# A message-passing layer on one core: a fourth scatter table, and the remainders of two of five dense groups made on VectorE

## The reference

```python
h = jnp.maximum(_layernorm(x, axis=-1), 0.0)
row, col = src, dst
msg = jnp.concatenate([h[col], edge_attr], axis=1)
msg = jnp.maximum(msg @ W1a + b1a, 0.0) @ W1b + b1b
summed = jax.ops.segment_sum(msg, row, num_segments=6250)
counts = jax.ops.segment_sum(ones, row, num_segments=6250)
agg = summed / jnp.maximum(counts, 1.0)[:, None]
out = x + jnp.maximum(jnp.concatenate([h, agg], axis=1) @ W2a + b2a, 0.0) @ W2b + b2b
```

## Time and profile before

| | |
|---|---|
| three timed runs, median (lowest, highest) | 1560.24 us (1558.22, 1563.16) |
| the profiled execution | 1549.54 us, span 1548.0 us |
| TensorE busy, matmuls | 1460.7 us (94%) x31106 |
| TensorE busy, weight loads | 1395.6 us (90%) |
| VectorE busy | 1413.5 us (91%) |
| ScalarE busy | 1027.4 us (66%) |
| GpSimd busy | 1214.8 us (78%) |
| granted TensorE clock, mean | 0.981 of full speed |

### The profile page before, as it was taken

The page is one execution under the profiler, slowest core; times in us unless marked ns, Lnnn a source line. Parts: engine busy times, 40 slices in busy tenths (PEclk is TensorE's granted clock), DMA queues, the critical chain, the costliest instruction groups (busy, mean ns, idle before and its releaser), DMA issues. The chain is left out here.

```text
span 1548.0 us, 76249 instructions
## 1 busy us (share of the span) xinstructions
PE 1460.7 (94%) x31106; PEld 1395.6 (90%) x31106; DVE 1413.5 (91%) x4756; ACT 1027.4 (66%) x2192; POOL 1214.8 (78%) x803
## 2 busy tenths in 40 slices
PE   3589999999999999999999999999999999999977
PEld 2368999999999999999999999999999999999975
DVE  8778999999999999999999999999999989999977
ACT  5287666776767676666667766666776666676605
POOL 4378888888788888888888888888888888888754
PEclk8699999999999999999999999999999999999998
DMA  5777767767677777777677767676676767677743
GB/s 167 268 135 129 121 111 113 124 113 122 108 125 111 125 112 113 121 107 125 110 123 113 124 110 115 115 122 112 112 123 113 119 104 125 112 119 114 116 82 110
DMA packets 279671, 187.44 MB, mean 121 GB/s; under 512 B 190687, under 2 KB 275548, under 8 KB 278553
## 3 DMA queue, kind: packets, MB, share of 16 engines
q1 hardware_dynamic: 174342, 153.22, 40.5%
q0 software_dynamic: 104976, 29.30, 27.8%
HBM read 148.22 MB, written 34.18 MB: 118 GB/s over the span
## 5 line engine op out<-in xcount | busy, mean ns | idle before, releaser
L525 POOL DMA_INDIRECT sums<-vv,sidx x726 | 1159.6, 1597 | 279.2 <-issue 199.6
L1256 PE MATMUL rank_ps<-area 128*128 128x64 bf16 (+1 forms) x21000 | 765.3, 193 | 9.9 <-issue 2.6
L1256 PEld LDWEIGHTS rank_ps<-area 128*128 128x128 bf16 x21000 | 729.0, 98 | 31.5 <-issue 17.3
L703 ACT ACTIVATE area<-rank_ps 64x392 bf16<-64x392 f32 x1400 | 685.1, 489 | 75.9 <-PE rank_ps L1242 49.5
L1242 PE MATMUL rank_ps<-r_d,oh 128*128 128x196 bf16 x4200 | 480.7, 249 | 4.8 <-DVE oh L936 2.9
L951 DVE TENSOR_SCALAR area<-iota,local 128x640 bf16<-128x640 int16 x1400 | 479.7, 406 | 4.9
L1242 PEld LDWEIGHTS rank_ps<-r_d,oh 128*128 128x128 bf16 x4200 | 343.9, 96 | 18.7 <-DVE oh L936 3.0
L936 DVE TENSOR_SCALAR oh<-iota,rank 128x640 bf16<-128x640 int16 x846 | 287.7, 406 | 0.0
L686 ACT ACTIVATE r_d<-z_ps 128x384 f32<-128x384 f32 x423 | 207.9, 491 | 82.4 <-PE z_ps L1212 72.1
L691 ACT ACTIVATE vv<-c_ps 128x396 f32<-128x396 f32 x121 | 60.7, 501 | 234.3 <-PE c_ps L1231 220.1
L958 DVE TENSOR_TENSOR dense<-rank_ps,dense 128x325 f32<-128x325 f32 x280 | 136.5, 487 | 80.4 <-PE rank_ps L1256 79.8
(11 more groups left out here) (130 smaller groups left out, 726.8 us busy)
## 6 DMA issues: line engine op xcount, KB each, us to landing
ids_s<-ids SPq DMA_DIRECT2D x248, 192.0 KB
et_d<-in_e_t SPq DMA_DIRECT2D x143, 192.0 KB
ids_d<-ids SPq DMA_DIRECT2D x143, 192.0 KB
et_s<-in_e_t SPq DMA_DIRECT2D x124, 192.0 KB
sums<-vv,sidx POOLq DMA_INDIRECT x726
sums<-dense POOLq DMA_DIRECT2D x3, 1657.5 KB
wp_d<-p_table SPq DMA_DIRECT2D x286, 15.8 KB
wp_s<-p_table SPq DMA_DIRECT2D x248, 15.8 KB
```

The source lines that it names most:

```text
L525: nc.gpsimd.indirect_dma_start(out=sums[t][:, :], out_offset=bass.IndirectOffsetOnAxis(ap=index, axis=0), in_=rows, in_offset=None, comput ...
L703: ins = nc.scalar.activation(routed[on, t.div(MACRO).mod(2), first:second + 1:second - first, t.mod(MACRO), :], bank[on, :, :], ACT.Copy)
L1256: ins = nc.tensor.matmul(l2_ps[h][:, u * W:u * W + w], oh2[:, g, u * P:(u + 1) * P], rows[:, PARTS[r]:PARTS[r] + w], start=g % MACRO == 0 ...
```

## The change

- There are four tables. Tile i goes to table i mod 4 up to tile 708; the last three sparse groups (18 tiles) use the first three tables only. When the fourth table is complete GpSimd signals `table_done`; SP, after its last loads, brings the table into the SBUF of `xc`, and VectorE adds it to `dense` in five pieces of 650 columns (`add_early`), four in the last cycles and one behind them. The tail adds three tables as before.
- For dense groups 1 to 5 and those with g mod 5 in (1, 3), VectorE makes the remainders (`split_dense`, between `hot` of the dense group and `add_sums` 0); TensorE's two `take_off` and ScalarE's second and third reading of these groups go. The counts of `split_ready` and `z_ready` follow from `read`.
- The two digit columns of a dense group's rows are copied by ScalarE (`keep_digits`) and no longer by VectorE (L933), but for the first group.
- The bias is added at the start of the third cycle (`add_bias`), not ahead of the tail.
- The tables are zeroed before GpSimd's `rest` and `low`, not after.
- A second path for inputs that don't fit, which does not run here, keeps three tables.

```diff
-TABLES = 3
+TABLES = 4
+ANY_TABLES = 3
+LATE = 3
+OPEN = (SPARSE - LATE) * TPG
+VECTOR = tuple(1 <= g <= MACRO or g % 5 in (1, 3) for g in range(DENSE + 1))
+VECTOR_UP_TO = tuple(sum(VECTOR[:g]) for g in range(DENSE + 1))
...
-        tab = [words(k * NTP * W, NTP * W) for k in range(TABLES)]
+        tab = [words(k * NTP * W, NTP * W) for k in range(TABLES - 1)]
+        early_tab = xc[:].rearrange("p t d -> p (t d)")[:, 0:NT * W]
...
-        READS = (1, 3)
+        def on_vector(kind, g):
+            return kind == S or VECTOR[g.base]
+        def read(kind, g, r):
+            return g.base + r + 1 if kind == S else 3 * g.base - 2 * VECTOR_UP_TO[g.base] + r + 1
+        def last_read(kind, g):
+            return read(kind, g, 0 if on_vector(kind, g) else 2)
...
# SP
+                sp.wait_ge(table_done, 1)
+                sp.dma_start(early_tab, sums[TABLES - 1][0:REAL, :].rearrange("(p t) w -> p (t w)", t=NT)).then_inc(early_in, 16)
                 sp.wait_ge(sums_done, 1)
                 sp.wait_ge(summed, done(PER * DENSE))
+                sp.wait_ge(slots_ready, done(DG))
...
# GpSimd
+                pool.wait_ge(zeros_ready, 1)
+                for k in range(TABLES):
+                    zero(k)
                 pool.sem_inc(rest_ready, START)
...
                 pipelined([(1, rest), (0, low)])
-                pool.wait_ge(zeros_ready, 1)
-                for k in range(TABLES):
-                    zero(k)
...
+                def table_of(tile):
+                    if tile < OPEN:
+                        return tile % TABLES, tile // TABLES
+                    late = tile - OPEN
+                    return late % (TABLES - 1), OPEN // TABLES + late // (TABLES - 1)
...
-                        t, before = tile.mod(TABLES), tile.div(TABLES)
-                        pool.wait_ge(scattered[t], before.times(16, 16))
+                        t, before = table_of(g.base * TPG + k)
+                        pool.wait_ge(scattered[t], 16 + 16 * before)
                         scatter_rows(k, t, sidx[:, slot, k:k + 1], vv[:, slot, k, 0:W])
+                        if g.base * TPG + k == OPEN + 3:
+                            pool.wait_ge(scattered[TABLES - 1], 16 + 16 * (OPEN // TABLES))
+                            pool.sem_inc(table_done, 1)
...
# ScalarE
+                    def keep_digits(g):
+                        act.wait_ge(slots_ready, done(1))
+                        nc.scalar.activation(rows3(DN, g)[:, :, DIG:DIG + 2],
+                                             digits.rearrange("p k g c -> p k (g c)")[:, :, bass.ds(g.times(2), 2)], ACT.Copy)
...
                             for f, r in enumerate((0, None, 1, None, 2)):
-                                if r is not None:
+                                if fit and f == 0:
+                                    keep_digits(t.plus(1))
+                                if r == 0 or r and not on_vector(DN, t.plus(1)):
                                     split(DN, t.plus(1), r)
                                 keep_routed(t, f)
...
# VectorE
+                def split_dense(g):
+                    dve.wait_ge(split_ready[DN], done(read(DN, g, 0)))
+                    rows = rows3(DN, g)
+                    for r in range(2):
+                        at = PARTS[r]
+                        if r:
+                            dve.wait_ge(dparts_ready, done(2 * VECTOR_UP_TO[g.base] + 1))
+                        nc.vector.tensor_tensor(rows[:, :, PARTS[r + 1]:PARTS[r + 1] + D], rows[:, :, at:at + D],
+                                                halves(DN, g)[:, :, at:at + D], ALU.subtract).then_inc(dparts_ready, 1)
...
                 def slots(t):
-                    nc.vector.tensor_copy(rows3(DN, t)[:, :, DIG:DIG + 2],
+                    if t.base == 0:
+                        nc.vector.tensor_copy(rows3(DN, t)[:, :, DIG:DIG + 2],
...
+                def add_early(k):
+                    if k == 0:
+                        dve.wait_ge(early_in, 16)
+                    part = slice(k * PER * BW, (k + 1) * PER * BW)
+                    dve.wait_ge(summed, done(PER * (DENSE - MACRO + k + 1)))
+                    nc.vector.tensor_tensor(dense[:, part], dense[:, part], early_tab[:, part], ALU.add).then_inc(early_added, 1)
+                def add_bias():
+                    b2b = rowb[:, 1:2, :].to_broadcast([P, NTP, D])
+                    nc.vector.tensor_tensor(xs[:], xs[:], b2b, ALU.add).then_inc(xb_ready, 1)
...
                     def cycle(s, n, t, routes, sums_too):
+                        if t.base == 2:
+                            add_bias()
...
                             hot(DN, t.plus(2))
+                        if routes and on_vector(DN, t.plus(1)):
+                            split_dense(t.plus(1))
                         if sums_too:
                             add_sums(now, 0)
...
+                        if now.base > DENSE - MACRO:
+                            add_early(now.base - 1 - (DENSE - MACRO))
                         if sums_too:
                             add_sums(now, 1)
...
                     cycles(cycle)
+                    add_early(MACRO - 1)
...
# VectorE, ahead of the tail
-                b2b = rowb[:, 1:2, :].to_broadcast([P, NTP, D])
-                nc.vector.tensor_tensor(xs[:], xs[:], b2b, ALU.add).then_inc(xb_ready, 1)
-                dve.wait_ge(pads_ready, TABLES)
+                dve.wait_ge(pads_ready, TABLES - 1)
+                dve.wait_ge(early_added, MACRO)
...
# TensorE
-                        pe.wait_ge(split_ready[DN], done(t.times(3, 3)))
+                        pe.wait_ge(split_ready[DN], done(last_read(DN, t)))
                         z(DN, t.plus(1))
+                        if on_vector(DN, t):
+                            pe.wait_ge(dparts_ready, done(2 * VECTOR_UP_TO[t.base] + 2))
                         route(t, 0)
                         sums_of(0)
                         route(t, 1)
-                        take_off(DN, t.plus(1), 0)
+                        if not on_vector(DN, t.plus(1)):
+                            take_off(DN, t.plus(1), 0)
...
-                        take_off(DN, t.plus(1), 1)
+                        if not on_vector(DN, t.plus(1)):
+                            take_off(DN, t.plus(1), 1)
```

More of the change, by code:

```diff
@@ L414, in refill @@
                         sp.sem_inc(sp_past, 1)
-                    sp.wait_ge(z_ready[kind], done(g.times(READS[kind], 1)))
+                    sp.wait_ge(z_ready[kind], done(read(kind, g, 0)))
                     sp.sem_inc(sp_past, 1)
@@ L558, in _ @@
                     cycles(cycle)
-                    for t in range(TABLES):
-                        pool.wait_ge(scattered[t], 16 * (1 + len(range(t, SPARSE * TPG, TABLES))))
+                    for k in range(TABLES - 1):
+                        t, before = table_of(SPARSE * TPG - 1 - k)
+                        pool.wait_ge(scattered[t], 32 + 16 * before)
                 with pool.Else():
@@ L605, in _ @@
                     cycles(cycle)
-                    for t in range(TABLES):
-                        pool.wait_ge(scattered[t], 16 * (1 + GROUPS * TPG // TABLES))
+                    for t in range(ANY_TABLES):
+                        pool.wait_ge(scattered[t], 16 * (1 + GROUPS * TPG // ANY_TABLES))
+                    pool.wait_ge(scattered[ANY_TABLES], 16)
                     pool.wait_ge(gathered[2], 16 * TPG * DG)
                     pool.wait_ge(dsrc_in, 16 * DG)
+                    pool.sem_inc(table_done, 1)
                 pool.sem_inc(sums_done, 1)
@@ L617, in _ @@
                     pool.wait_ge(tables_in, done(m + 1))
-                    for k in range(1, TABLES):
-                        if k > 1:
-                            pool.wait_ge(pool_part, done(m * (TABLES - 2) + k - 1))
-                        nc.gpsimd.tensor_tensor(tab[0][:, part], tab[0][:, part], tab[k][:, part],
-                                                ALU.add).then_inc(pool_sum if k == TABLES - 1 else pool_part, 1)
+                    nc.gpsimd.tensor_tensor(tab[0][:, part], tab[0][:, part], tab[1][:, part], ALU.add).then_inc(pool_part, 1)
+                    pool.wait_ge(pool_part, done(m + 1))
+                    nc.gpsimd.tensor_tensor(tab[0][:, part], tab[0][:, part], tab[2][:, part], ALU.add).then_inc(pool_sum, 1)
             @block.scalar
@@ L893, in hot @@
                     if g.base >= 2:
-                        dve.wait_ge(z_ready[kind], done(g.plus(-2).times(READS[kind], 1)))
+                        dve.wait_ge(z_ready[kind], done(read(kind, g.plus(-2), 0)))
                     dst = ids_s[:, slot, 1, :] if kind == S else ids_d[:, slot, :]
@@ L1086, in general @@
                     cycles(cycle)
+                    for m in range(MACRO):
+                        add_early(m)
                 fit = dve.value_load(fits_i[0:1, 0:1], min_val=0, max_val=1)
@@ L1216, in take_off @@
                 def take_off(kind, g, r):
```

(2 more changed lines are left out.)

36 lines of the change are left out of this document (20 added, 16 removed).

## The result

| | before | after |
|---|---|---|
| timed runs, median (lowest, highest) | 1560.24 us (1558.22, 1563.16) | 1550.0 us (1549.98, 1550.43) |
| the profiled execution, its span | 1548.0 us | 1548.7 us |
| TensorE idle in its body | 15.7 us | 33.6 us |
| VectorE idle in its body | 90.5 us | 37.4 us |

The ratio of the timed runs is 0.9931, interval [0.9916, 0.9945]: 0.7% faster, where 1548 us was predicted. But the two profiled executions have the same length. What the timed runs gained can't be seen between these two traces, and that was the first thing to explain.

What follows compares the result with a forecast made beforehand. TensorE was taken to set the pace, with VectorE close behind. Terms -10 + 0 + 0 + 0.5 - 2.6 = -12.1 us against the profiled 1549.5, with 10.7 us carried over to timed runs, gave 1548 us, range 1537 to 1562.

Steps and rivals of the forecast that it cites:

- Set-up and first cycles: Before the body: first cycles cost 0 (-2 to +3.5 us); zeroing the tables earlier costs 0 (-1.5 to +3).
- The body, -10: The 135 body cycles: TensorE saves 18.4 us, 8 come back; net -10 us, bounds -18.4 to 0.
- I take 0.4: 8 us back: Body: late VectorE costs TensorE 0 to 0.8 us at each of 19 cycles without a sparse group; 0.4 taken.
- The 1.2 us of play before a short cycle: Body: VectorE's `slots` can be 1.2 us late before a cycle without a sparse group, 2.7 otherwise.
- relief is eaten: Rival, 0.20: short cycles cost 1 us each, blocked VectorE waits last 1.2 us; body gains 0, 1556 to 1562 us.
- its own sign: Body: prediction is wrong if TensorE's idle time rises by more than 18 us or doesn't rise at all.
- Nobody waits for those now, so the gain is nothing directly: GpSimd's scatter waits: the fourth table gains nothing itself, only lets GpSimd follow if other engines get faster.
- 22 us, between 0 and 44.1: GpSimd's queue: how much of its 44.1 us of waits for the previous scatter into the same table can go.
- Carrying the 10.7 us over: Whole kernel: the timed median's 10.7 us above the profiled execution was assumed to remain after the change.
- Last cycles and tail, -2.1: End of kernel: early table addition costs +0.5 us (0 to +2), removing the tail's bias addition gives -2.6 (-3.5 to -1.5).
- GpSimd held up by the subtractions (0.02): Rival, 0.02: each of 118 new VectorE subtractions holds up scatters by its 0.5 us; 1585 us.
- VectorE becomes the bound, slower: Rival, 0.13: in the body over 30 of VectorE's 76 us of waits stay; with 40 left, 1568 us.

Runs made afterwards that it cites:

- placed: The kernel after, with groups for VectorE's remainders chosen around the 19 cycles without a sparse group (62 groups, not 59); second chip: 1524.78 us, 0.9771 of the kernel before.
- before_look: The kernel before, unchanged, on the second chip for a second profile: one run, 1555.87 us.
- split_alone: The kernel before with only the dense remainders of the 59 groups moved to VectorE, three tables kept; first chip: 1564.55 us, 1.0047 of the kernel before.
- no_vector: The kernel after, but with no dense remainders made on VectorE; first chip: 1551.27 us, 0.9957 of the kernel before.
- table_alone: The kernel before with only the fourth table and its early addition; second chip: 1522.73 us, 0.9756 of the kernel before.
- after_third: The kernel after, unchanged, on the second chip: 1533.75 us, 0.9841 of the kernel before.
- no_vector_2: The kernel after without dense remainders on VectorE, run on the second chip: 1524.17 us, 0.9769 of the kernel before.

## Why the prediction was right in its number, and where it failed

*Set-up and first cycles, 0 (-2 to +3.5, and -1.5 to +3).* Set-up: the first dense edge matmul at 79.32 against 80.00, the wait for the window load gone as expected. First cycles: 2.2 us longer, inside the bounds; how much of that is the addition, which takes 3.6 us, isn't shown.

*The body, -10.* It failed: the body came out 1.0 us longer. The ledger took 18.4 us off TensorE, which was right (16.9 fewer busy), added 45.9 to VectorE (54.0 busy; a pair counts 2 x 0.554 us busy where 1.05 were taken from start to start, which is 3 of the 8), and gave back 8 at the short cycles. In the profiled body TensorE's idle time rose by 17.9 us. The step that failed reads "I take 0.4: 8 us back": the short cycles cost 15.1 us, 0.8 for each of the 19, twice what was taken and near the upper bound of 1. The other 2.8 us of idle time are small gaps elsewhere that the sum had no term for: -16.9 + 15.1 + 2.8 = +1.0. The 1.2 us of play before a short cycle was counted from a VectorE that is on time. A pair ahead of a short cycle, on top of a lag left by another, is more than that. That it is a matter of place and not of work is what placed shows: three pairs more, and little more than a third of the waits. The rival "relief is eaten" described the body; its other half, that a blocked wait of VectorE's lasts 1.2 us whatever its cause, wasn't tested. By its own sign, idle time up by more than 18 us, the prediction stood at the very edge.

*"Nobody waits for those now, so the gain is nothing directly."* This is the step that failed worst, and the number came out right by luck, since a second error stood against it. The waits of GpSimd for its landings were priced at nothing since ScalarE waited for GpSimd 4.3 us in the profile. That row was true of its one execution, which ran 10.7 us faster than the timed ones. before_look shows 187.6 us of that wait, and 23.1 us of TensorE's behind it. split_alone shows what happens if one takes work from TensorE and leaves the three tables: slower. no_vector prices the table with the small edits at 7.4 us where TensorE stalls (the tail gives 2.3 us of its own, see below, which leaves about 5 for the table), and table_alone prices it at 39 where it doesn't. So "nothing directly" is refuted on the second chip, and on the first it is off by up to 5 us. ScalarE's wait behind it was seen in the kernel before on the second chip alone; on the first it was seen in split_alone, 107.5 us, where the remainders are moved too. That the waits themselves would go was foreseen: 22 us, between 0 and 44.1, and 32.7 measured.

*Carrying the 10.7 us over.* The sum of -12.1 was made against 1549.5 and then moved up by the difference between the profiled and the timed executions. That difference was not a constant beside the kernel: the kernel after, timed at 1550.0, has a profiled execution of 1550.43. What it was is argued and not shown. GpSimd's hold on ScalarE in most executions of before, which the fourth table would end, fits; but on the first chip the table and the small edits gave 7.4 us, 2.3 of them in the tail. So -12.1 came out as about 0 against the profiled execution, and the offset of 10.7 that was carried over went. The two errors are of one size by accident. That the missing 10.7 us were this wait rests on before_look, a profile of the second batch, where TensorE doesn't stall; where it does, no execution of before as long as the timed ones was profiled.

*Last cycles and tail, -2.1.* The last cycles took 1502.74 - 1468.70 = 34.04 us against 1499.62 - 1466.17 = 33.45, so +0.6 where 0.5 was predicted. The tail gave 8.4 - 6.1 = 2.3 us against 2.6; the additions were estimated at 0.83 us and took 0.827. The Trainium skill, SBUF — State Buffer, "SBUF: two separate sides", has a VectorE instruction with two inputs in SBUF and a GpSimd instruction that reads SBUF exclude each other for a whole instruction; the 3.184 us that fell to 0.941 at most agrees.

*GpSimd held up by the subtractions (0.02).* Not by an amount that counts: the mean of a scatter is 1.612 us with 118 more subtractions beside them and 1.597 without, 726 x 0.015 = 11 us in all at the most where 59 were feared, and ScalarE never waits for GpSimd in that trace. But the mechanism exists. Two-input additions in f32 do hold up a scatter, as the 4.87 us beside the bias addition show; 3.3 of the 11 us are that one scatter, and the subtractions are too short (0.55 us each) to do much. The prediction had the bias addition at 3.56 us in the third cycle and no term for what it does to GpSimd. The Trainium skill, SBUF — State Buffer, same section, warns that GpSimd can't write descriptors while VectorE holds the shared ports in its two-port modes; for the subtractions the trace shows no hold-up of their own length, for the long addition it does.

*"VectorE becomes the bound, slower" (0.13).* On the first chip no. On the second it half holds: VectorE idles 25.5 us of 1240 in after_third, is late 23 times, and the remainders cost 9.6 us, while the whole change is faster even so. A chance for it was right, though its reason was the total of VectorE's work; placed, with more work and without the loss, shows that the play in the short cycles decides.

## What to carry to other kernels

Where the profiled execution is faster than every timed one, its waits are not those of the kernel: take a second profile before a wait is priced at nothing, and don't add the difference to a forecast as if it were a constant. A wait that nobody stands behind today (GpSimd's 44 us for its landings) is a bound a few microseconds away; relieve it first, and only then move work off the engine in front. When work is moved to an engine with little spare time, choose the cycles for it by their play and not by an even pattern: 54 pairs cost 30.6 us of waits in one order, 57 cost 11.2 in another.

## What the runs showed of the hardware

TensorE's block of 75 short matmuls, 31 ns each, has a stall of about 0.2 us in it in most cycles of all traces of the first batch and hardly ever in those of the other two, for the same kernels too: 2.57 against 2.33 us in the blocks above. It falls at varying places in the block, after the 68th weight load in the one shown. A kernel that keeps TensorE full took 1551.27 us where it stalls and 1524.17 where it doesn't (no_vector, no_vector_2), 27 us less; the kernel before took 1558.67 and 1559.66, the same. Its cause wasn't found, and whether it belongs to the chip or to how the program was loaded stays open, since each chip had its own batches; table_alone and placed weren't run where it stalls, so which version is best there isn't known.

A scatter that starts inside a long two-input f32 addition of VectorE's is held until the addition is over: seven times of seven it ended 1.4 us behind the addition, and took 3.2 to 4.9 us in place of 1.6.

An indirect scatter of 128 rows occupies GpSimd for 1.91 us from start to start, 1.6 for itself and 0.3 for the gap, with nothing to wait for. 726 of them are 1385 us, and in the fastest kernels here that is the bound.
